# Layer 0 feed-forward on one core: rows normalised and scaled by ACT a tile ahead, first butterfly level taken by PE in pairs of blocks

## The chip, the core and the metric

The kernel runs on one core of a Trainium2 chip, as one launch. The metric is the device time of that launch in microseconds (us), lower being better. The engines are PE (TensorE, the matrix engine), DVE (VectorE), ACT (ScalarE), POOL (GpSimd) and SP (SyncE, which here only issues transfers). Each engine works through its own instructions in order. Engines wait for one another by semaphores that count up.

## What is computed

The whole kernel is four pairs of layers on x, 16 tiles of 128 rows by 256 columns. Each layer adds its result to x. This case is about the second of the eight, the feed-forward of layer 0, with a Hadamard transform and 8-bit quantised activations:

```python
def act_quant(x):                      # per row
    scale = 128 / clip(max(abs(x)), 1e-5)
    return clip(round(x * scale), -128, 127) / scale
def fwht(x):                           # over 1024 columns, h = 1, 2, 4, ... 512
    a, b = (x[..., 0, :], x[..., 1, :])
    x = stack([a + b, a - b])          # at each of ten levels
    return x / sqrt(1024)
n = layernorm(x)
gate = act_quant(n) @ weight_quant(w_gate).T      # 256 -> 1024
up   = act_quant(n) @ weight_quant(w_up).T
x = x + act_quant(fwht(silu(gate) * up)) @ weight_quant(w_down).T   # 1024 -> 256
```

The ten levels of the transform split in two: seven inside a block of 128 columns (one product with a 128x128 matrix of plus and minus ones, `had`), and three across the eight blocks (sums and differences of whole blocks, the "butterflies").

## The kernel before, in words

`hadamard_ffn` (from L1266 on) is the stage of this layer. It takes one tile of 128 rows after another, t = 0 to 15, in a pipeline that is written out by hand: each engine has a function `tile(t, u)` that lists what it does for which tile, and runs it for t = 0 to 15 (`over_long_pipe`; the last four tiles are written out, because there the work ahead falls away). u is t modulo 2 and picks one of two buffers. `ahead(t, n)` is true where tile t + n exists. What each engine does in its tile t, in this order:

- **DVE**: `quantise_x(t+3)`, which is normalise (L221), row maximum (L1348), its scale (L1350), reciprocal (L1352), `deq` (L1355), times the reciprocal plus a rounding constant (L1358), clip to bf16 (L1362); `gate_times_up(t+2)` (L1369, writes `prod`); `scale_h(t)`, which is the row maximum of the transformed tile in PSUM (L1374) and its scales down to the reciprocal `b_rec` (L1380); `add_to_x(t-1)` (L1390 and the row statistics, L193); `quantise_h(t)` (L1386).
- **ACT**: `copy_mixedT(t)` in two halves (L1434), `silu(t+2)` (L1428), `copy_hqT(t-1)` in two halves (L1447), `copy_xqT(t+3)` (L1421), `round_h(t)` (L1440).
- **PE**: `turn_mixed(t, 0)` (L1502), gate product of t+2 (L1491), `turn_mixed(t, 1)`, up product of t+2, `transform(t)` in two halves (L1511) with `turn_hq(t-1)` (L1526) behind each half, `turn_xq(t+3)` (L1480), `down(t-1)` (L1534).
- **POOL**: `butterflies(t)`: three levels of two instructions each (L1336, L1337), on halves of 128x512, prod to fly to prod to mixed.

The waits that matter below. `down(t-1)` waits until ACT has copied the turned rows of t+3 (`xqT_done`), since both use one bank of PSUM. `turn_mixed(t, 1)` waits for `copy_mixedT(t, 0)`, as there is one `ps_t`. `transform(t)` waits for both `copy_mixedT(t)` and for `round_h(t-1)`, as there is one `ps_f`. `scale_h(t)` waits for `had_put` of t. `add_to_x(t-1)` waits for `down(t-1)`.

Before the first tile POOL computes the reciprocal deviations of all 16 tiles (`all_rstd`, L216), then clears `zeros` and sets `magic`. DVE quantises rows 0, 1 and 2 between the first products.

Of the kernel before, what the change touches and what calls it, by code (L numbers as in the profile page):

```python
# [8 lines left out]
P = 128  # L9
# [49 lines left out]
        body(t, t % 2)  # L59


def over_ring(eng, body, n, ring, lead=1):

    rest = n % ring or ring
    for j in range(lead * ring):
        body(j, j % ring)
    with eng.Fori(lead, (n - rest) // ring) as i:
        for r in range(ring):
            body(i * ring + r, r)
    for j in range(n - rest, n):  # L70
# [25 lines left out]
class Core:  # L96


    def __init__(self, nc, ctx, dram):
# [32 lines left out]
        self.had = self.sb("had_matrix", [P, P], F32, self.early)  # L132
# [1133 lines left out]
def hadamard_ffn(core, name):  # L1266
# [3 lines left out]
    with core.stage() as st:  # L1270
        def sb(n, shape, dt=F32):
            return core.sb(f"{name}_{n}", shape, dt, st)

        def sem(n):
            return core.sem(f"{name}_{n}", st)
# [6 lines left out]
        xn = sb("xn", [P, D])  # L1282
        xq = sb("xq", [P, D], BF16)
        xqT = [sb(f"xqT{u}", [P, KC, P], BF16) for u in range(2)]
        a_max, a_rec = sb("a_max", [P, 1]), sb("a_rec", [P, 1])
# [5 lines left out]
        fly = sb("fly", [P, FF])  # L1291
# [19 lines left out]
        rstd_done = sem("rstd_done")  # L1311
        zeroed = sem("zeroed")
        block = st.enter_context(nc.Block())

# [5 lines left out]

        @block.gpsimd
        def _(pool):
            all_rstd(pool, core, rstd_done)
            pool.memset(core.zeros[:, :], 0.0).then_inc(zeroed, 1)
            pool.memset(magic[:, :], MAGIC).then_inc(const_done, 1)

            def butterflies(t, u):

                pool.wait_ge(prod_done, t + 1)
                if after(t, 2):  # L1330
                    pool.wait_ge(mixT_put, t - 1)
                for n, (src, dst) in enumerate(((prod[u], fly), (fly, prod[u]), (prod[u], mixed[u]))):
                    v, o = (m[:, :].rearrange("p (a two c) -> p a two c", two=2, c=P << n) for m in (src, dst))
                    if n:
                        pool.drain()
                    pool.tensor_tensor(o[:, :, 0, :], v[:, :, 0, :], v[:, :, 1, :], ALU.add)  # L1336
                    last = pool.tensor_tensor(o[:, :, 1, :], v[:, :, 0, :], v[:, :, 1, :], ALU.subtract)  # L1337
                last.then_inc(mixed_done, 1)

            over_tiles(pool, butterflies)  # L1340

        @block.vector
        def _(dve):
            def quantise_x(t, u):
                dve.drain()
                normalise(dve, core, xn[:, :], t)
                dve.drain()
                dve.tensor_reduce(a_max[:, :], xn[:, :], AX.X, ALU.max, apply_absolute_value=True)  # L1348
                dve.drain()
                dve.tensor_scalar(a_max[:, :], a_max[:, :], 1e-5, 1.0 / 128, ALU.max, ALU.mult)  # L1350
                dve.drain()
                dve.reciprocal(a_rec[:, :], a_max[:, :])  # L1352
                if after(t, 2):
                    dve.wait_ge(silu_done, t - 1)
                dve.tensor_scalar(deq[u][:, :], w_mean[:, 0:2], a_max[:, :], None, ALU.mult)\  # L1355
                   .then_inc(deq_done, 1)
                dve.drain()
                dve.tensor_scalar(xn[:, :], xn[:, :], a_rec[:, :], MAGIC, ALU.mult, ALU.add)  # L1358
                dve.drain()
                if after(t, 1):  # L1360
                    dve.wait_ge(xqT_put, t)
                dve.tensor_scalar(xq[:, :], xn[:, :], MAGIC, 127.0, ALU.subtract, ALU.min).then_inc(xq_done, 1)  # L1362

            def gate_times_up(t, u):
                dve.wait_ge(silu_done, t + 1)
                dve.wait_ge(up_put, t + 1)
                if after(t, 2):
                    dve.wait_ge(mixed_done, t - 1)
                dve.scalar_tensor_tensor(out=prod[u][:, :], in0=ps_u[:, :], scalar=deq[u][:, 1:2], in1=gate[:, :],  # L1369
                                         op0=ALU.mult, op1=ALU.mult).then_inc(prod_done, 1)  # L1370

            def scale_h(t, u):
                dve.wait_ge(had_put, t + 1)
                dve.tensor_reduce(b_max[:, :], ps_f[:, :], AX.X, ALU.max, apply_absolute_value=True)  # L1374
                dve.drain()

                dve.tensor_scalar(b_max[:, :], b_max[:, :], 32 * EPS_Q, 1.0 / 128, ALU.max, ALU.mult)
                dve.drain()
                dve.tensor_scalar(b_deq[u][:, :], b_max[:, :], w_mean[:, 2:3], 1.0 / 32, ALU.mult, ALU.mult)
                dve.reciprocal(b_rec[:, :], b_max[:, :]).then_inc(b_scale, 1)  # L1380

            def quantise_h(t):
                dve.wait_ge(round_done, t + 1)
                if after(t, 1):
                    dve.wait_ge(hqT_put, 2 * t)
                dve.tensor_scalar(hq[:, :], rounded[:, :], MAGIC, 127.0, ALU.subtract, ALU.min).then_inc(hq_done, 1)  # L1386

            def add_to_x(t, u):
                dve.wait_ge(y_put, t + 1)
                dve.scalar_tensor_tensor(out=core.xt(t), in0=ps_y, scalar=b_deq[u][:, :], in1=core.xt(t),  # L1390
                                         op0=ALU.mult, op1=ALU.add).then_inc(x_done, 1)
                dve.drain()
                row_stats(dve, core, t)

            def tile(t, u):
                if ahead(t, 3):
                    quantise_x(t + 3, 1 - u)
                if ahead(t, 2):
                    gate_times_up(t + 2, u)
                scale_h(t, u)  # L1400
                if after(t, 1):
                    add_to_x(t - 1, 1 - u)
                quantise_h(t)

            dve.wait_ge(rstd_done, 1)
            quantise_x(0, 0)
            quantise_x(1, 1)
            gate_times_up(0, 0)
            quantise_x(2, 0)
            gate_times_up(1, 1)  # L1410
            over_long_pipe(dve, tile)
            add_to_x(B - 1, 1)
            finish_stats(dve, core)

        @block.scalar
        def _(act):
# [55 lines left out]
        def _(pe):  # L1472
# [32 lines left out]
            def transform(t, half):  # L1505
# [1203 lines left out]
def lay_out(np, a):  # L2709
# [75 lines left out]
```

## Time and profile before

| | us |
|---|---|
| median of 3 runs | 1629.64 (1629.09 to 1630.54) |
| the profiled execution, its own time | 1628.51 |
| its span in the profile | 1626.7 |
| mean granted clock of TensorE, share of full | 0.936 |
| busy in the span: PE, DVE, ACT, POOL | 1352.0, 1071.2, 777.4, 631.9 |

The span is the time from the first to the last instruction of the profiled execution. The rest of its own time lies around it. A busy engine need not be what bounds a stage: what bounds it is read from which instruction starts as soon as which other one ends. "[x <-E y]" at the end of a row says that the engine had been idle for x us before it, until engine E had written y. Full clock of TensorE is 2.4 GHz; a granted clock of 0.50 is 1.2 GHz.

### The profile page before, as it was taken

How to read it: one execution, taken by the hardware profiler on the slowest of the kernel's cores; microseconds unless marked ns; L12 is line 12 of the kernel's file. 1: busy time of each engine (PE TensorE's matmuls, PEld its weight loads, DVE VectorE, ACT ScalarE, POOL GpSimd, SP SyncE). 2: the span in 40 equal slices, each digit the busy share in tenths (PEclk: the TensorE clock that was granted, in tenths of full speed). 3: DMA queues.
4: the chain of work that ended last, by engine and by line, in shares of the span. 5: the costliest groups of instructions: out<-in, count | busy, mean ns of one | idle time of the engine just before them, and what ended most of it. 6: DMA issues, size and time to landing. Idle time of an engine off the chain costs nothing. (4 is left out here: it accounts for less than half of the span.)

```text
span 1626.7 us, 29297 instructions
## 1 busy us (share of the span) xinstructions
PE 1352.0 (83%) x7976; PEld 845.5 (52%) x7992; DVE 1071.2 (66%) x2429; ACT 777.4 (48%) x2322; POOL 631.9 (39%) x649
## 2 busy tenths in 40 slices
PE   3899996566759969799997999978995999978993
PEld 2555553345534434476554666554663666654662
DVE  3898896788748855422664888875334888864224
ACT  2676773344540025432105888842442788833330
POOL 3112420777757523474002112112444665214661
PEclk9999997899979959999997999998998999998997
DMA  4231001400010022397501000141442210411224
GB/s 151 76 83 48 17 15 62 149 0 0 1 52 0 0 84 75 109 303 222 157 1 48 25 28 22 49 159 43 133 128 74 65 49 29 172 55 56 84 84 162
DMA packets 96447, 124.80 MB, mean 77 GB/s; under 512 B 11117, under 2 KB 76464, under 8 KB 96112
## 3 DMA queue, kind: packets, MB, share of 16 engines
q1 hardware_dynamic: 85392, 95.63, 18.5%
q0 software_dynamic: 10608, 28.07, 5.9%
q8 instruction: 36, 0.59, 0.1%
q14 instruction: 43, 0.35, 0.1%
q10 hardware_dynamic: 368, 0.16, 0.0%
HBM read 91.31 MB, written 33.43 MB: 77 GB/s over the span
## 5 line engine op out<-in xcount | busy, mean ns | idle before, releaser
L695 ACT ACTIVATE l0a_prob<-l0a_ps_s,l0a_neg_max 128x128 f32<-128x128 f32 x512 | 137.6, 398 | 67.7 <-DVE l0a_neg_max L553 60.0
L695 ACT ACTIVATE l2a_prob<-l2a_ps_s,l2a_neg_max 128x128 f32<-128x128 f32 x512 | 138.3, 399 | 26.7 <-DVE l2a_neg_max L553 21.7
L1135 ACT ACTIVATE l3a_prob<-l3a_ps_s,l3a_neg_max 128x256 f32<-128x256 f32 x256 | 104.3, 482 | 33.9 <-DVE l3a_neg_max L1050 32.3
L216 POOL TENSOR_TENSOR ln_rstd<-ln_var_eps,minus_half 128x16 f32<-128x16 f32 x7 | 20.5, 2922 | 233.5 <-POOLq L171 207.0
L553 DVE TENSOR_REDUCE l2a_neg_max<-l2a_ps_s 128x4 f32<-128x512 f32 x128 | 85.5, 683 | 19.1 <-PE l2a_ps_s L793 18.1
L501 POOL TENSOR_TENSOR l2a_k_head<-l2a_kT,head_of_row 128x512 f32<-128x512 f32 x32 | 32.9, 1047 | 161.7 <-DMA l2a_kT<-k_rows 161.7
L562 DVE COPY l0a_probT<-l0a_ps_t 128x512 f32<-128x512 f32 x128 | 84.4, 680 | 15.4 <-PE l0a_ps_t L805 15.2
L1050 DVE TENSOR_REDUCE l3a_neg_max<-l3a_ps_s 128x2 f32<-128x512 f32 x128 | 84.0, 679 | 14.2 <-PE l3a_ps_s L1186 13.0
L553 DVE TENSOR_REDUCE l0a_neg_max<-l0a_ps_s 128x4 f32<-128x512 f32 x128 | 85.2, 681 | 10.4 <-PE l0a_ps_s L793 9.6
L1748 PE MATMUL l1a_ps_y<-l1a_kv,l1a_tap 128*128 128x512 f32 x192 | 84.3, 602 | 3.7 <-POOL l1a_kv L1720 3.7
L501 POOL TENSOR_TENSOR l0a_k_head<-l0a_kT,head_of_row 128x512 f32<-128x512 f32 x30 | 30.8, 1047 | 145.6 <-DMA l0a_kT<-k_rows 145.6
L805 PE MATMUL l2a_ps_t<-ident,l2a_prob 128*128 128x128 f32 x512 | 75.6, 281 | 8.0 <-DVE l2a_probT L562 7.0
L805 PEld LDWEIGHTS l2a_ps_t<-ident,l2a_prob 128*128 128x128 f32 x512 | 56.7, 142 | 42.5 <-DVE l2a_probT L562 24.7
L2607 PE MATMUL l3f_ps_g<-l3f_w_gu_all,l3f_xinT 128*128 x156 | 73.5, 593 | 0.0
L805 PE MATMUL l0a_ps_t<-ident,l0a_prob 128*128 128x128 f32 x512 | 69.9, 273 | 1.8 <-DVE l0a_probT L562 1.8
L1198 PE MATMUL l3a_ps_t<-ident,l3a_prob 128*128 128x128 f32 x512 | 69.1, 278 | 2.2 <-ACT l3a_probT L1143 2.0
L1720 POOL TENSOR_TENSOR l1a_kv<-l1a_vT,ctxT_all 128x1024 f32 (+1 forms) x32 | 61.6, 1947 | 18.8 <-PE l1a_ps_y L1748 18.5
L2297 DVE TENSOR_TENSOR l3f_h_sb<-l3f_ps_g,l3f_act_sb 128x256 f32<-128x256 f32 x39 | 16.5, 424 | 77.9 <-ACT l3f_act_sb L2453 77.9
L562 DVE COPY l2a_probT<-l2a_ps_t 128x512 f32<-128x512 f32 x96 | 64.6, 681 | 4.4 <-PE l2a_ps_t L805 4.4
L783 PE MATMUL l0a_ps_s<-l0a_mask,identb 128*128 128x512 bf16 x128 | 49.7, 397 | 21.0 <-ACT l0a_prob L695 21.0
L2071 POOL DMA_INDIRECT l2f_xin<-expert_rows,l2f_tokens x47 | 44.6, 949 | 55.4 <-PE l2f_ps_x L2593 42.1
L1198 PEld LDWEIGHTS l3a_ps_t<-ident,l3a_prob 128*128 128x128 f32 x512 | 56.9, 142 | 17.1 <-ACT l3a_probT L1143 10.9
(477 smaller groups left out, 3532.4 us busy)
## 6 DMA issues: line engine op xcount, KB each, us to landing
l1f_w_gu<-in_l1f_w_gu SPq DMA_DIRECT2D x32, 352.0 KB, 6.8
expert_results<-zeros SPq DMA_DIRECT2D x1, 8320.0 KB, 26.3
l1f_got<-expert_results SPq DMA_DIRECT2D x16, 512.0 KB, 3.9
expert_results<-l2f_y_sb SPq DMA_DIRECT2D x47, 128.0 KB, 1.7
l1f_w_d<-in_l1f_w_d SPq DMA_DIRECT2D x32, 176.0 KB
l2f_w_gu_all<-in_l2f_w_gu SPq DMA_DIRECT2D x1, 4096.0 KB, 15.2
l3f_w_gu_all<-in_l3f_w_gu SPq DMA_DIRECT2D x1, 4096.0 KB, 15.4
l3f_got<-expert_results SPq DMA_DIRECT2D x16, 256.0 KB, 5.0
```

The costliest lines, as they stand in the source:

```text
L501: pool.tensor_tensor(k_head[u][:, c, :, :], kT[u][:, c:c + 1, :].broadcast_to([P, R, P]), core.head_of_row[:, :].unsqueeze(2).broadcast_to ...
L553: dve.tensor_reduce(neg_max[:, j, :], ps_s[j][:, :].rearrange("p (r k) -> p r k", r=R), AX.X, ALU.max, negate=True).then_inc(max_done, 1)
L562: dve.tensor_copy(probT[4 * c + j][:, :], ps_t[j % 2][:, :]).then_inc(t_done_v, 1)
L695: last = act.activation(prob[4 * c + j][:, r * P:r * P + P], ps_s[j][:, r * P:r * P + P], ACT.Exp, bias=neg_max[:, j, r:r + 1])
L783: pe.matmul(ps_s[j][:, :].rearrange("p (r k) -> p r k", r=R), core.identb[:, :], mask[u][:, :].unsqueeze(1).broadcast_to([P, R, P]), start ...
L805: last = pe.transpose(ps_t[j % 2][:, r * P:r * P + P], prob[4 * c + j][:, r * P:r * P + P], core.ident[:, :])
L1050: dve.tensor_reduce(neg_max[:, j, :], ps_s[j][:, :].rearrange("p (r k) -> p r k", r=2), AX.X, ALU.max, negate=True).then_inc(max_done, 1)
L1135: last = act.activation(prob[4 * c + j][:, m * D:m * D + D], ps_s[j][:, m * D:m * D + D], ACT.Exp, bias=neg_max[:, j, m:m + 1])
L1198: last = pe.transpose(ps_t[j % 2][:, k * D + m * P:k * D + m * P + P], prob[4 * c + j][:, m * D + k * P:m * D + k * P + P], core.ident[:, :])
L1720: pool.tensor_tensor(kv[u][:, c, :].rearrange("p (b j i) -> p b j i", b=B, i=N8), i_rows, j_rows, ALU.mult).then_inc(kv_done, 1)
L1748: last = pe.matmul(ps[u][c][:, cols], tap[u][:, (c - m) * P:(c - m) * P + P], kv[u][:, m, cols], start=(m == 0), stop=(m == c))
L2607: last = pe.matmul(ps_g[r % 2][:, 0:2 * FE], xinT[r % 2][:, c, :], w, start=(c == 0), stop=(c == KC - 1))
```

## The change

The normalising and the scaling of the rows move from DVE to ACT (`norm` writes `xn` a tile further ahead, `round_x` writes `xr`). DVE keeps the measuring (`measure_x`) and the clip (`clip_x`), which are put at other places of its tile. On POOL the level over neighbouring blocks goes; on PE each product with `had` has 256 columns in place of 128 and writes a pair of blocks, the second of the pair added to the first. POOL's first instruction is split, the first three tiles ahead of the rest. The long pipe has six tiles written out at its end in place of four.

```diff
@@ butterflies (POOL)
-                for n, (src, dst) in enumerate(((prod[u], fly), (fly, prod[u]), (prod[u], mixed[u]))):
+                for n, (src, dst) in ((1, (prod[u], fly[u])), (2, (fly[u], mixed[u]))):
...
@@ DVE
+            def shifts(lo, hi):
+                dve.scalar_tensor_tensor(out=shift[:, lo:hi], in0=core.stats[:, lo:hi, 0], scalar=-1.0, in1=core.rstd[:, lo:hi],
+                                         op0=ALU.mult, op1=ALU.mult).then_inc(shift_done, 1)
+            def measure_x(t, u):
+                dve.wait_ge(normed, t + 1)
+                dve.tensor_reduce(a_max[u][:, :], xn[u][:, :], AX.X, ALU.max, apply_absolute_value=True)
+                dve.drain()
+                dve.tensor_scalar(a_max[u][:, :], a_max[u][:, :], 1e-5, 1.0 / 128, ALU.max, ALU.mult)
+                dve.drain()
+                dve.reciprocal(a_rec[:, :], a_max[u][:, :]).then_inc(x_scaled, 1)
+                dve.tensor_scalar(deq[u][:, :], w_mean[:, 0:2], a_max[u][:, :], None, ALU.mult)\
                    .then_inc(deq_done, 1)
-                dve.drain()
-                dve.tensor_scalar(xn[:, :], xn[:, :], a_rec[:, :], MAGIC, ALU.mult, ALU.add)
-                dve.drain()
+            def clip_x(t):
+                dve.wait_ge(x_rounded, t + 1)
                 if after(t, 1):
                     dve.wait_ge(xqT_put, t)
-                dve.tensor_scalar(xq[:, :], xn[:, :], MAGIC, 127.0, ALU.subtract, ALU.min).then_inc(xq_done, 1)
+                dve.tensor_scalar(xq[:, :], xr[:, :], MAGIC, 127.0, ALU.subtract, ALU.min).then_inc(xq_done, 1)
...
             def tile(t, u):
-                if ahead(t, 3):
-                    quantise_x(t + 3, 1 - u)
                 if ahead(t, 2):
                     gate_times_up(t + 2, u)
                 scale_h(t, u)
+                if ahead(t, 3):
+                    clip_x(t + 3)
                 if after(t, 1):
                     add_to_x(t - 1, 1 - u)
+                if ahead(t, 4):
+                    measure_x(t + 4, u)
                 quantise_h(t)
...
@@ ACT
+            def norm(t, u):
+                act.activation(xn[u][:, :], core.xt(t), ACT.Identity, bias=shift[:, bass.ds(t, 1)],
+                               scale=core.rstd[:, bass.ds(t, 1)]).then_inc(normed, 1)
+            def round_x(t, u):
+                act.wait_ge(x_scaled, t + 1)
+                if after(t, 1):
+                    act.wait_ge(xq_done, t)
+                act.activation(xr[:, :], xn[u][:, :], ACT.Identity, bias=magic[:, :], scale=a_rec[:, :])\
+                    .then_inc(x_rounded, 1)
...
                 if ahead(t, 3):
                     copy_xqT(t + 3, 1 - u)
                 round_h(t)
+                if ahead(t, 4):
+                    round_x(t + 4, u)
+                if ahead(t, 5):
+                    norm(t + 5, 1 - u)
...
@@ PE, transform
                 for c in range(half * NF // 2, (half + 1) * NF // 2):
-                    last = pe.matmul(ps_f[:, c * P:c * P + P], mixedT[:, c * P:c * P + P], had[:, :], start=True, stop=True)
+                    odd = c % 2
+                    pair = slice((c - odd) * P, (c - odd + 2) * P)
+                    last = pe.matmul(ps_f[:, pair], mixedT[:, c * P:c * P + P], had[:, odd * P:(odd + 2) * P],
+                                     start=(odd == 0), stop=(odd == 1))
...
@@ lay_out
-    o["had"] = had
+    o["had"] = np.concatenate([had, had, -had], axis=1)
```

Before the pipe, in the new kernel, DVE measures and clips rows 0, 1 and 2 and measures row 3, and ACT norms rows 0 to 4 and rounds rows 0 to 3, between their copies and silus.

## Rows read from the trace of the kernel before

**Rows 1.** A steady stretch: us, each engine busy us (instructions), clock, DMA, GB/s
```profile
350.00:360.00 10.00, 6.42 (x52) 4.75 (x51) 8.53 (x16) 4.87 (x7) 7.92 (x7) 1.00 0.00 0
```

**Rows 2.** Timeline, DVE: start us, duration us; the maximum that opens scale_h
```profile
303.16 1.21 DVE L1374 TENSOR_REDUCE l0f_b_max<-l0f_ps_f 128x1 f32<-128x1024 f32 x1
...
354.02 1.21 DVE L1374 TENSOR_REDUCE l0f_b_max<-l0f_ps_f 128x1 f32<-128x1024 f32 x1
364.01 1.22 DVE L1374 TENSOR_REDUCE l0f_b_max<-l0f_ps_f 128x1 f32<-128x1024 f32 x1
...
424.29 1.21 DVE L1374 TENSOR_REDUCE l0f_b_max<-l0f_ps_f 128x1 f32<-128x1024 f32 x1
...
438.89 1.23 DVE L1374 TENSOR_REDUCE l0f_b_max<-l0f_ps_f 128x1 f32<-128x1024 f32 x1 [3.22 <-PE l0f_ps_f L1511]
```

**Rows 3.** Timeline, 351 to 361 us: work removed or moved, and what follows it
```profile
351.12 1.26 POOL L1337 TENSOR_TENSOR l0f_mixed<-l0f_prod 128x512 f32<-128x512 f32 x1
351.29 1.25 DVE L1358 TENSOR_SCALAR l0f_xn<-l0f_xn,l0f_a_rec 128x256 f32<-128x256 f32 x1
352.62 0.29 DVE L1362 TENSOR_SCALAR l0f_xq<-l0f_xn 128x256 bf16<-128x256 f32 x1
352.82 1.28 DVE L1369 SCALAR_TENSOR_TENSOR l0f_prod<-l0f_ps_u,l0f_deq,l0f_gate 128x1024 f32<-128x1024 f32 x1
353.89 1.03 PE L1534 MATMUL l0f_ps_q<-w_int,l0f_hqT 128*128 128x256 bf16 x8 [0.56 <-ACT l0f_xqT L1421]
354.18 1.26 POOL L1336 TENSOR_TENSOR l0f_fly<-l0f_prod 128x512 f32<-128x512 f32 x1 [1.79 <-DVE l0f_prod L1369]
...
355.67 0.15 DVE L1380 RECIPROCAL l0f_b_rec<-l0f_b_max 128x1 f32<-128x1 f32 x1
...
356.81 1.27 POOL L1336 TENSOR_TENSOR l0f_prod<-l0f_fly 128x512 f32<-128x512 f32 x1
...
358.99 0.92 DVE L221 TENSOR_SCALAR l0f_xn<-x_rows,ln_mean_var,ln_rstd 128x256 f32 x1 [0.36 <-issue]
...
359.98 0.42 DVE L1348 TENSOR_REDUCE l0f_a_max<-l0f_xn 128x1 f32<-128x256 f32 x1
...
360.70 0.17 DVE L1352 RECIPROCAL l0f_a_rec<-l0f_a_max 128x1 f32<-128x1 f32 x1
```

**Rows 4.** Timeline, last tiles, where DVE no longer quantises rows ahead
```profile
429.23 1.15 PE L1511 MATMUL l0f_ps_f<-had_matrix,l0f_mixedT 128*128 128x128 f32 x8
430.20 1.28 DVE L1369 SCALAR_TENSOR_TENSOR l0f_prod<-l0f_ps_u,l0f_deq,l0f_gate 128x1024 f32<-128x1024 f32 x1 [1.30 <-ACT l0f_gate L1428]
...
434.54 0.59 ACT L1434 ACTIVATE l0f_mixedT<-l0f_ps_t 128x512 f32<-128x512 f32 x1
...
436.52 1.16 PE L1511 MATMUL l0f_ps_f<-had_matrix,l0f_mixedT 128*128 128x128 f32 x8 [0.69 <-ACT l0f_mixedT L1434]
...
439.76 1.05 PE L1534 MATMUL l0f_ps_q<-w_int,l0f_hqT 128*128 128x256 bf16 x8 [0.69 <-ACT l0f_hqT L1447]
...
441.43 0.43 DVE L193 BATCH_NORM_STATS2 ln_partial<-x_rows 128x6 f32<-128x256 f32 x1
```

**Rows 5.** Instructions of a tile, next stage: ACT's norm, duration ns min/median/max
```profile
L1663 ACT ACTIVATE l1a_xn<-x_rows,l1a_shift,ln_rstd x16: 587/592/602, 460.3 to 476.3; 128x256 f32<-128x256 f32 x16
```

**Rows 6.** Last stage, fp32, 256 columns: one record, ns min/median/max; four, timeline
```profile
L2629 PE MATMUL l3f_ps_l<-l3f_w_d_all,l3f_hT_sb x152: 379/379/479, 1488.0 to 1599.0; 128*128 x152
...
1506.10 1.03 PE L2629 MATMUL l3f_ps_l<-l3f_w_d_all,l3f_hT_sb 128*128 x4
```

**Rows 7.** Stretches before and in a low clock, and the product in it
```profile
402.00:404.00 2.00, 0.28 (x2) 0.11 (x2) 1.92 (x3) 0.68 (x2) 0.54 (x1) 1.00 0.00 0
404.00:406.00 2.00, 1.96 (x10) 1.53 (x11) 1.85 (x5) 0.00 (x0) 1.58 (x2) 0.50 0.00 0
...
404.05 1.86 PE L1534 MATMUL l0f_ps_q<-w_int,l0f_hqT 128*128 128x256 bf16 x8 [0.57 <-ACT l0f_xqT L1421]
```

**Rows 8.** Timeline, the first transform of the stage
```profile
297.69 2.04 PE L1511 MATMUL l0f_ps_f<-had_matrix,l0f_mixedT 128*128 128x128 f32 x16
```

More of the change, by code:

```diff
@@ L59, in over_long_pipe, with over_x_pipe @@
         body(t, t % 2)
+def over_x_pipe(eng, body):
+    body(0, 0)
+    body(1, 1)
+    with eng.Fori(1, B // 2 - 3) as i:
+        body(i * 2, 0)
+        body(i * 2 + 1, 1)
+    for t in range(B - 6, B):
+        body(t, t % 2)
 def over_ring(eng, body, n, ring, lead=1):
@@ L90 @@
 READY = 3
+FIRST = 3
 RING = 4
@@ L131, in __init__ @@
         self.ffn_raw = [self.sb(f"ffn_raw{n}", [P, KC * FF], F32, self.early) for n in range(3)]
-        self.had = self.sb("had_matrix", [P, P], F32, self.early)
+        self.had = self.sb("had_matrix", [P, 3 * P], F32, self.early)
         self.w_int = [self.sb(f"w_int{n}", [P, KC * FF], BF16, self.early) for n in range(3)]
@@ L216, in all_rstd, with rstd_in_parts @@
     pool.tensor_tensor(core.rstd[:, :], core.var_eps[:, :], core.minus_half[:, :], ALU.pow).then_inc(done, 1)
+def rstd_in_parts(pool, core, done):
+    for part in (slice(0, FIRST), slice(FIRST, B)):
+        pool.tensor_tensor(core.rstd[:, part], core.var_eps[:, part], core.minus_half[:, part], ALU.pow).then_inc(done, 1)
 def normalise(dve, core, out, b):
@@ L1281, in hadamard_ffn @@
         magic = sb("magic", [P, 1])
-        xn = sb("xn", [P, D])
+        xn = [sb(f"xn{u}", [P, D]) for u in range(2)]
+        xr = sb("xr", [P, D])
+        shift = sb("shift", [P, B])
         xq = sb("xq", [P, D], BF16)
         xqT = [sb(f"xqT{u}", [P, KC, P], BF16) for u in range(2)]
-        a_max, a_rec = sb("a_max", [P, 1]), sb("a_rec", [P, 1])
+        a_max, a_rec = [sb(f"a_max{u}", [P, 1]) for u in range(2)], sb("a_rec", [P, 1])
         deq = [sb(f"deq{u}", [P, 2]) for u in range(2)]
@@ L1290, in hadamard_ffn @@
         prod = [sb(f"prod{u}", [P, FF]) for u in range(2)]
-        fly = sb("fly", [P, FF])
+        fly = [sb(f"fly{u}", [P, FF]) for u in range(2)]
         mixed = [sb(f"mixed{u}", [P, FF]) for u in range(2)]
@@ L1310, in hadamard_ffn @@
              "had_put", "b_scale", "round_done", "hq_done", "hqT_put", "hqT_done", "y_put", "x_done"))
-        rstd_done = sem("rstd_done")
+        rstd_done, shift_done, normed, x_scaled, x_rounded = (sem(n) for n in (
+            "rstd_done", "shift_done", "normed", "x_scaled", "x_rounded"))
         zeroed = sem("zeroed")
@@ L1322, in _ @@
         def _(pool):
-            all_rstd(pool, core, rstd_done)
+            rstd_in_parts(pool, core, rstd_done)
             pool.memset(core.zeros[:, :], 0.0).then_inc(zeroed, 1)
@@ L1331, in butterflies @@
                     pool.wait_ge(mixT_put, t - 1)
-                for n, (src, dst) in enumerate(((prod[u], fly), (fly, prod[u]), (prod[u], mixed[u]))):
+                for n, (src, dst) in ((1, (prod[u], fly[u])), (2, (fly[u], mixed[u]))):
                     v, o = (m[:, :].rearrange("p (a two c) -> p a two c", two=2, c=P << n) for m in (src, dst))
-                    if n:
+                    if n > 1:
                         pool.drain()
@@ L1343, in _ @@
         def _(dve):
-            def quantise_x(t, u):
+            def shifts(lo, hi):
[4 more added lines that the diff above has]
+                dve.tensor_reduce(a_max[u][:, :], xn[u][:, :], AX.X, ALU.max, apply_absolute_value=True)
                 dve.drain()
-                normalise(dve, core, xn[:, :], t)
+                dve.tensor_scalar(a_max[u][:, :], a_max[u][:, :], 1e-5, 1.0 / 128, ALU.max, ALU.mult)
                 dve.drain()
-                dve.tensor_reduce(a_max[:, :], xn[:, :], AX.X, ALU.max, apply_absolute_value=True)
-                dve.drain()
-                dve.tensor_scalar(a_max[:, :], a_max[:, :], 1e-5, 1.0 / 128, ALU.max, ALU.mult)
-                dve.drain()
[L1352 to L1355, printed above, removed]
+                dve.reciprocal(a_rec[:, :], a_max[u][:, :]).then_inc(x_scaled, 1)
+                dve.tensor_scalar(deq[u][:, :], w_mean[:, 0:2], a_max[u][:, :], None, ALU.mult)\
                    .then_inc(deq_done, 1)
-                dve.drain()
-                dve.tensor_scalar(xn[:, :], xn[:, :], a_rec[:, :], MAGIC, ALU.mult, ALU.add)
-                dve.drain()
+            def clip_x(t):
+                dve.wait_ge(x_rounded, t + 1)
                 if after(t, 1):
                     dve.wait_ge(xqT_put, t)
-                dve.tensor_scalar(xq[:, :], xn[:, :], MAGIC, 127.0, ALU.subtract, ALU.min).then_inc(xq_done, 1)
+                dve.tensor_scalar(xq[:, :], xr[:, :], MAGIC, 127.0, ALU.subtract, ALU.min).then_inc(xq_done, 1)
             def gate_times_up(t, u):
@@ L1400, in tile @@
                 scale_h(t, u)
+                if ahead(t, 3):
+                    clip_x(t + 3)
                 if after(t, 1):
                     add_to_x(t - 1, 1 - u)
+                if ahead(t, 4):
+                    measure_x(t + 4, u)
                 quantise_h(t)
             dve.wait_ge(rstd_done, 1)
-            quantise_x(0, 0)
-            quantise_x(1, 1)
+            shifts(0, FIRST)
+            measure_x(0, 0)
+            clip_x(0)
+            dve.wait_ge(rstd_done, 2)
+            shifts(FIRST, B)
+            measure_x(1, 1)
+            clip_x(1)
             gate_times_up(0, 0)
-            quantise_x(2, 0)
+            measure_x(2, 0)
+            clip_x(2)
             gate_times_up(1, 1)
-            over_long_pipe(dve, tile)
+            measure_x(3, 1)
+            over_x_pipe(dve, tile)
             add_to_x(B - 1, 1)
@@ L1459, in tile @@
                 round_h(t)
+                if ahead(t, 4):
+                    round_x(t + 4, u)
+                if ahead(t, 5):
+                    norm(t + 5, 1 - u)
+            act.wait_ge(shift_done, 1)
+            norm(0, 0)
+            norm(1, 1)
             act.wait_ge(const_done, 1)
+            round_x(0, 0)
+            round_x(1, 1)
             copy_xqT(0, 0)
+            norm(2, 0)
             copy_xqT(1, 1)
             silu(0, 0)
+            round_x(2, 0)
+            act.wait_ge(shift_done, 2)
+            norm(3, 1)
             copy_xqT(2, 0)
             silu(1, 1)
-            over_long_pipe(act, tile)
+            round_x(3, 1)
+            norm(4, 0)
+            over_x_pipe(act, tile)
             copy_hqT(B - 1, 0)
```

## The prediction

> **What bounds the kernel now.** Only the feed-forward of layer 0 changes, so its stage is read first by busy time and then in order of time. In a steady stretch of 10 us DVE is busy 8.53, POOL 7.92, PE 6.42 and ACT 4.87 us, at full clock [rows 1]. The maximum that opens `scale_h` comes once a tile, so its starts give the period: 354.02 to 364.01 is 10.0 us, and from 303.16 (tile 0) to 424.29 (tile 12) it is 121.1 us, 10.1 a tile [rows 2]. In these tiles DVE goes from one instruction to the next; it waits for nobody but shortly for `round_h`. Part of its time is lost to POOL: L1358 starts at 351.29 and ends at 352.54, and POOL's instruction beside it ends at 352.38, 0.16 us earlier [rows 3]. So DVE sets the period, its waits for POOL included. In the last tiles, where it quantises no rows ahead, the period is (438.89 - 424.29) / 2 = 7.3 us, and there DVE waits 3.22 us for the transform [rows 2]: the second bound is the chain transform, maximum, `round_h`, transform. From 303.16 to the start for tile 15 it is 135.7 + 7.3 = 143.0 us.
>
> **What is taken away.** DVE loses the normalise, 0.92 us, and the scaling, 1.25 us [rows 3], a tile: 2.2 us of 10. POOL loses two of six instructions of 1.26, so it can't bind. ACT gets two more instructions. The nearest row is `norm` of the next stage, the same operation on the same shape: 0.59 us [rows 5]. It has 4.87 + 1.18 = 6.05 us of work then, so by busy time it has room. By busy time alone the change would win. But the order in which the pieces were put back decides.
>
> **The new chain.** I follow what waits for what from the maximum of tile t to that of t+1, with time 0 at its start.
> - `b_rec` ends at 355.82 - 354.02 = 1.80 [rows 2, 3].
> - Only now comes `clip_x(t+3)` on DVE, 0.29 us, so 2.09 if nothing holds it. It stood ahead of `scale_h` before.
> - Does POOL hold it? POOL's work starts behind `gate_times_up(t+2)`, which starts when `silu` is done, 430.20 - 429.23 = 0.97 after the transform's start, and takes 1.28 [rows 4]. POOL follows 0.08 later; its third instruction starts 356.81 - 354.18 = 2.63 behind the first and takes 1.27 [rows 3]. So it ends 6.23 us after the transform's start, and the clip, 0.16 behind it as L1358 was, at 6.39.
> - The transform. Each of its 16 records a tile goes from 128 to 256 columns. 16 took 2.04 [rows 8]; at 256 columns four took 1.03 and one 0.38, so the step is (1.03 - 0.38) / 3 = 0.217 and 16 take 3.63 [rows 6]. That is 1.6 more. From its start to the maximum it was 438.89 - 436.52 = 2.37 [rows 2, 4]; it becomes 3.97. The clip ends at 6.39 - 3.97 = 2.42.
> - `turn_xq(t+3)`, the copy `copy_xqT(t+3)`, then `down(t-1)`, which waits for that copy: from the clip's end to the start of `down` 353.89 - 352.91 = 0.98 [rows 3]. At 3.40.
> - `down(t-1)` and then `add_to_x(t-1)` with its statistics: 441.86 - 439.76 = 2.10 [rows 4]. At 5.50. Before, this lay beside DVE's queue and cost nothing; its cover was the rows work that stood ahead.
> - `measure_x(t+4)` is queued behind it: maximum to reciprocal 360.87 - 359.98 = 0.89 [rows 3], and 0.07 of gap. At 6.46.
> - `round_x(t+4)` waits for that, in ACT's order behind `round_h(t)`, and behind it are `norm(t+5)` and `copy_mixedT(t+1, 0)`. 0.05 + 2 x 0.59 = 1.23. At 7.69. This is the added wait that matters: all of ACT's next tile is queued behind it, and PE's second `turn_mixed` and its transform wait for ACT.
> - From `copy_mixedT(t+1, 0)` to the next transform 436.52 - 434.54 = 1.98 [rows 4]. At 9.67.
> - The transform, 3.97. The next maximum starts at **13.64**.
>
> Each link is an order of one engine or a semaphore, and each comes once in a tile, so the period can't be under this sum at these prices, however free DVE is. The period of 10.0 becomes 13.6.
>
> **The sum.** Tiles 0 to 10: 11 x 13.64 = 150.0. Tile 11 has no `norm` behind it, 13.05. Tile 12 has the clip but no `round_x`: `down` ends at 4.43, `turn_mixed` at about 5.0 (half of the tile's product of 1.15 [rows 4]), then 1.98 and 3.97: 11.0. Tiles 13 and 14: 7.3 + 1.6 = 8.9 each. Together 191.9 against 143.0: +48.9. Before the pipe: the first transform ended at 299.73 and its maximum started at 303.16 [rows 2, 8], held by the rows of tile 3 on DVE. That 3.4 goes, 1.6 of wider products and up to 1.2 for `round_x(3)` and `norm(4)` ahead of ACT's first copy come, and the clips of the first rows are held less; -4 to +1, I take -2. The split of POOL's first instruction and DVE's `shifts` are in this bound. Longer buffers and the larger `had` load lie far ahead and cost nothing: the load is issued in an earlier stage.
>
> The clock. In 402 to 404 PE had 0.28 us of work, and from 404 on the granted clock was 0.50, the 1.2 GHz level; `down` then took 1.86 in place of 1.03 [rows 3, 7]. It cost nothing there, as DVE set the period. Now PE idles twice in a tile: from the transform's end to `down` (0 to 3.4, but for 0.28 of work), and from the gate product (about 6) until ACT's copy is done (8.3). I expect one fall a tile, seen on `down`: 0.83 x 12 = +10. Bounds: 0 where the clock holds; 0.83 and half of a transform at half speed, 1.8, so 2.6 a tile, +32.
>
> +48.9 - 2 + 10 = +57 on the profiled execution's 1628.5: 1685.4. The median of the runs is 1.1 above that execution, so **1686** for the median.
>
> What the Trainium skill would put here: "TensorE: Matmul & The Clock Gate", section "Wait — 56ns, not 53.3ns?", has back-to-back products N / 2.4 GHz + 2.5 ns apart, and the footnote of "Perfetto Trace Analysis" halves the rate for fp32 in two parts. By that a record goes from 112 to 218 ns, 1.7 us a tile in place of 1.6, since the pages leave out the weight load beside it. It would make the sum some 1.5 us larger. The 0.217 of the row agrees with its 218.
>
> **The rivals.**
> - *DVE's relief comes through* (chance 0.06). ACT would have to be let go early: `x_scaled` of t+4 at or before the end of `round_h(t)`, about 4.5 (clip end 2.42, copy done about 3.3, `round_h` 1.2), and not at 6.46. Then the chain is clip, copy, `round_h`, transform: 4.5 + 3.97 = 8.5. 12 x (8.5 - 10.1) = -19, three last tiles at +1.6, -2 before the pipe: -16, so 1614. For it speaks that DVE is the busiest engine now. It decides only if the part from `down` to `copy_mixedT` loses over 3.6 us of its length, which is where the period passes 10.0; the order written in `tile` speaks against that. "SBUF — State Buffer", section "Who interferes with whom", of the Trainium skill says that ACT never waits for another engine's port, which speaks for this side: the two instructions moved there lose their waits for POOL. The trace's even 587 to 602 ns of `norm` agrees [rows 5]. It says nothing of the queue.
> - *The clock holds* (0.20): the same chain without the 10, 1676.
> - *The clock falls in both gaps* (0.15): +32 in place of +10, 1708.
> - *A shorter chain* (0.07): the clip finds POOL between instructions (-0.3 a tile), `round_x` and `norm` overlap or take less (-0.4), or wide products cost half of what I take, all at full clock: 12 x 1 to 1.5 less than 1676, 1658 to 1664.
> - *No difference* (0.02): the two sides would have to cancel.
>
> The forecast itself has 0.50. The range is 1665 to 1708: the forecast with the bounds of its unknown prices and both clock rivals. Changes of 0.2% (3.3 us) are about the least that a measurement of this kernel can tell. Faster 0.06, within 0.02, slower 0.92.
>
> **What would show it.** Right: maxima (L1374 before) about 13.6 to 14.5 us apart, DVE idle before them with the transform as releaser; ACT idle some 2 us before `round_x` on the reciprocal; DVE idle before `add_to_x` on `down`; DVE's busy time a tile near 6 us; 16 records of 256 columns in 3.6 us. The stage longer, every other stage as before. Wrong: a period under 10, or ACT's `round_x` with no idle time before it, would refute the chain. A granted clock of 1.0 throughout the stage gives the second rival.

## The result, and the profile of the changed kernel

The changed kernel took 1688.41 us (median of 4 runs, 1678.55 to 1695.31) against 1629.91 before: a ratio of 1.0344, 95% interval [1.0298, 1.0391]. The forecast was 1686. The profiled execution took 1691.74 us with a span of 1690.0 (before 1628.51 and 1626.7).

First the steady part of the stage, from the first maximum (tile 0) to that of tile 11 in the changed kernel, and to that of tile 12 in the one before. The columns are stretch, its length, busy time and instructions of PE, PE's weight loads, DVE, ACT and POOL, then granted clock, DMA share, GB/s.

```profile
301.28:465.02 163.74, 116.62 (x542) 78.81 (x542) 64.77 (x141) 63.57 (x98) 56.41 (x46) 0.79 0.01 4
```

That is 163.74 / 11 = 14.9 us a tile, where the kernel before took 10.1. The kernel before:

```profile
303.16:424.29 121.13, 81.85 (x582) 60.50 (x595) 104.02 (x180) 58.44 (x84) 96.34 (x74) 0.94 0.00 0
```

DVE worked 104.02 / 12 = 8.7 us a tile and now 64.77 / 11 = 5.9: the relief came. POOL went from 8.0 to 5.1, ACT from 4.9 to 5.8. No engine is short of time, and the tile is 4.8 us longer. PE's busy share is no measure here: its busy time grew with wide products and with the low clock (0.79 in place of 0.94). Now the starts of the maximum that opens `scale_h`, DVE's timeline:

```profile
301.28 1.22 DVE L1395 TENSOR_REDUCE l0f_b_max<-l0f_ps_f 128x1 f32<-128x1024 f32 x1 [1.49 <-PE l0f_ps_f L1569]
314.67 1.23 DVE L1395 TENSOR_REDUCE l0f_b_max<-l0f_ps_f 128x1 f32<-128x1024 f32 x1 [3.09 <-PE l0f_ps_f L1569]
328.12 1.23 DVE L1395 TENSOR_REDUCE l0f_b_max<-l0f_ps_f 128x1 f32<-128x1024 f32 x1 [1.68 <-PE l0f_ps_f L1569]
342.29 1.22 DVE L1395 TENSOR_REDUCE l0f_b_max<-l0f_ps_f 128x1 f32<-128x1024 f32 x1 [1.68 <-PE l0f_ps_f L1569]
356.80 1.23 DVE L1395 TENSOR_REDUCE l0f_b_max<-l0f_ps_f 128x1 f32<-128x1024 f32 x1 [1.68 <-PE l0f_ps_f L1569]
372.99 1.22 DVE L1395 TENSOR_REDUCE l0f_b_max<-l0f_ps_f 128x1 f32<-128x1024 f32 x1 [2.70 <-PE l0f_ps_f L1569]
...
465.02 1.22 DVE L1395 TENSOR_REDUCE l0f_b_max<-l0f_ps_f 128x1 f32<-128x1024 f32 x1 [2.93 <-PE l0f_ps_f L1569]
...
508.99 1.22 DVE L1395 TENSOR_REDUCE l0f_b_max<-l0f_ps_f 128x1 f32<-128x1024 f32 x1 [5.19 <-PE l0f_ps_f L1569]
```

These answer to [rows 2]. The first periods are 13.4, 13.5 and 14.2 us, later ones 14.5 and 16.2 by turns. DVE is idle ahead of each maximum and is released by the transform; before it was so in the last two tiles alone. From the first to the last maximum it is 508.99 - 301.28 = 207.7 us against 143.0; that and the earlier start, 301.28 against 303.16, make +62.8 of the 63.3 us by which the span grew. The other stages kept their length.

One tile in order of time, 328.12 to 342.29, the chain that the prediction built from [rows 3] and [rows 4]:

```profile
329.24 1.26 POOL L1357 TENSOR_TENSOR l0f_mixed<-l0f_fly 128x512 f32<-128x512 f32 x1
...
329.78 0.15 DVE L1401 RECIPROCAL l0f_b_rec<-l0f_b_max 128x1 f32<-128x1 f32 x1
329.86 0.79 DVE L1383 TENSOR_SCALAR l0f_xq<-l0f_xr 128x256 bf16<-128x256 f32 x1
...
331.10 0.38 ACT L1462 ACTIVATE l0f_xqT<-l0f_ps_q 128x256 bf16<-128x256 bf16 x1 [2.16 <-PE l0f_ps_q L1536]
331.62 1.57 PE L1593 MATMUL l0f_ps_q<-w_int,l0f_hqT 128*128 128x256 bf16 x8 [0.56 <-ACT l0f_xqT L1462]
...
333.36 0.48 DVE L1411 SCALAR_TENSOR_TENSOR x_rows<-l0f_ps_q,l0f_b_deq,x_rows 128x256 f32 x1 [2.72 <-PE l0f_ps_q L1593]
...
335.08 0.16 DVE L1375 RECIPROCAL l0f_a_rec<-l0f_a_max 128x1 f32<-128x1 f32 x1
...
335.28 0.60 ACT L1455 ACTIVATE l0f_xr<-l0f_xn,l0f_magic,l0f_a_rec 128x256 f32<-128x256 f32 x1 [2.70 <-DVE l0f_a_rec L1375]
335.79 0.58 ACT L1448 ACTIVATE l0f_xn<-x_rows,l0f_shift,ln_rstd 128x256 f32 x1
336.28 0.57 ACT L1475 ACTIVATE l0f_mixedT<-l0f_ps_t 128x512 f32<-128x512 f32 x1
...
337.60 0.60 ACT L1475 ACTIVATE l0f_mixedT<-l0f_ps_t 128x512 f32<-128x512 f32 x1 [0.75 <-PE l0f_ps_t L1558]
...
338.26 1.98 PE L1569 MATMUL l0f_ps_f<-had_matrix,l0f_mixedT 128*128 128x256 f32 x8
```

What to see is that one link follows the other without a break, across engines. The clip lasts until POOL's third instruction is done (329.24 to 330.50) and ends at 330.65, `down` starts at 331.62, the sum into x at 333.36, behind it the reciprocal of the rows ahead ends at 335.24, ACT's `round_x` has been idle for 2.70 us and starts at 335.28, `norm` follows, then the first copy of the turned tile at 336.28, and PE's transform at 338.26. Two of the longest waits of the stage (engine, tile, releaser, total us, times, longest):

```profile
DVE x_rows L1411 <- PE l0f_ps_q L1593: 34.8, 12, 3.1
...
ACT l0f_xr L1455 <- DVE l0f_a_rec L1375: 31.6, 11, 3.1
```

The second is the new one: 11 tiles, some 2.9 us each, with all of ACT's next tile queued behind it.

### The profile page after: what moved, and what is told of

Read it like the earlier page. It is cut to its first block and busy times, and to the rows that moved or that the text cites. A ratio compares the mean times of both kernels' runs of the same rounds, so it can differ in the third digit from the quotient of the medians.

```text
span 1690.0 us, 29216 instructions
## 1 busy us (share of the span) xinstructions
PE 1407.5 (83%) x7991; PEld 875.8 (52%) x7992; DVE 1029.5 (61%) x2399; ACT 793.2 (47%) x2354; POOL 586.9 (35%) x618
## 5 line engine op out<-in xcount | busy, mean ns | idle before, releaser
L713 ACT ACTIVATE l2a_prob<-l2a_ps_s,l2a_neg_max 128x128 f32<-128x128 f32 x512 | 138.3, 401 | 26.3 <-DVE l2a_neg_max L571 21.5
L580 DVE COPY l0a_probT<-l0a_ps_t 128x512 f32<-128x512 f32 x128 | 84.4, 680 | 15.4 <-PE l0a_ps_t L823 15.3
L1357 POOL TENSOR_TENSOR l0f_fly<-l0f_prod 128x512 f32<-128x512 f32 x16 | 20.2, 1266 | 134.6 <-DVE l0f_prod L1390 134.6
L1569 PE MATMUL l0f_ps_f<-had_matrix,l0f_mixedT 128*128 128x256 f32 x256 | 64.9, 398 | 1.4 <-ACT l0f_mixedT L1475 1.4
## 6 DMA issues: line engine op xcount, KB each, us to landing
l2f_w_gu_all<-in_l2f_w_gu SPq DMA_DIRECT2D x1, 4096.0 KB, 14.5
l3f_w_gu_all<-in_l3f_w_gu SPq DMA_DIRECT2D x1, 4096.0 KB, 14.9
```

The costliest lines, as they stand in the source:

```text
L580: dve.tensor_copy(probT[4 * c + j][:, :], ps_t[j % 2][:, :]).then_inc(t_done_v, 1)
L713: last = act.activation(prob[4 * c + j][:, r * P:r * P + P], ps_s[j][:, r * P:r * P + P], ACT.Exp, bias=neg_max[:, j, r:r + 1])
L1569: last = pe.matmul(ps_f[:, pair], mixedT[:, c * P:c * P + P], had[:, odd * P:(odd + 2) * P], start=(odd == 0), stop=(odd == 1))
```

## The experiments

The chips differ in the time of the kernel before (1631.6, 1650.2 and 1635.2 us, medians, for the three groups of four), so what is compared is the ratio to the runs of before beside it. "Stage" is the time from the first to the sixteenth maximum in the profile, 143.0 us before and 207.7 after. The chain theory says that the order of the pieces sets the period. Its rival says that the work added to PE and ACT does.

**One link taken out.** DVE measures ahead of the sum into x.

```diff
-                if after(t, 1):
-                    add_to_x(t - 1, 1 - u)
                 if ahead(t, 4):
                     measure_x(t + 4, u)
+                if after(t, 1):
+                    add_to_x(t - 1, 1 - u)
```

> One swap in the changed kernel: DVE measures the rows of t+4 before it adds tile t-1 to x. Chain theory: the reciprocal then comes about 3.4 us after the maximum instead of 6.5, ACT's round_h ends at 4.5, round_x and norm at 5.7, so the period at full clock goes from 13.6 to about 11.7 us and the time from 1688 to about 1666 us (the same loss to the clock). Rival, that PE's wider products and its low clock set the time and not the order: no change, 1680 to 1695 us.

Measured 1665.69 us, ratio 1.0201 [1.0134, 1.0267], stage 175.8, periods of 11.3 and 12.6 by turns, granted clock in the stage 0.91. ACT's timeline:

```profile
403.36 1.20 ACT L1481 ACTIVATE l0f_rounded<-l0f_ps_f,l0f_magic,l0f_b_rec 128x1024 f32<-128x1024 f32 x1
404.45 0.60 ACT L1455 ACTIVATE l0f_xr<-l0f_xn,l0f_magic,l0f_a_rec 128x256 f32<-128x256 f32 x1
404.94 0.59 ACT L1448 ACTIVATE l0f_xn<-x_rows,l0f_shift,ln_rstd 128x256 f32 x1
405.43 0.59 ACT L1475 ACTIVATE l0f_mixedT<-l0f_ps_t 128x512 f32<-128x512 f32 x1
```

No idle time is left ahead of L1455: `round_x`, `norm` and the copy follow `round_h` without a break. The periods of 11.3 are those at full clock, a little under the 11.7 expected. Two swapped lines gave back 22 us. Part of that can be the clock (0.82 in the first profile of the changed kernel), but not all: with the clock at 0.99 the old order still takes 189.2 us for the stage (last run of this part), 13.4 more than this one. So the rival, no change, is refuted.

**ACT's rows a tile later.** They stand behind `silu` of the next tile; the two that stood ahead of the pipe, for tiles 3 and 4, go, as the pipe now does them.

```diff
                     silu(t + 2, u)
+                if ahead(t, 3):
+                    round_x(t + 3, 1 - u)
+                if ahead(t, 4):
+                    norm(t + 4, u)
...
                 round_h(t)
-                if ahead(t, 4):
-                    round_x(t + 4, u)
-                if ahead(t, 5):
-                    norm(t + 5, 1 - u)
```

> ACT's round_x and norm move from the end of its tile to behind silu of the next tile, where their input has been ready for long; nothing else. Chain theory: ACT copies the turned tile as soon as round_h and PE's turn_mixed (behind down) are done, period about 11.0 us at full clock, 1688 - 12 x 2.6 = about 1657 us. Rival, that PE's wider products and its low clock set the time: no change, 1680 to 1695 us.

Measured 1661.30 us, ratio 1.0181 [1.0108, 1.0254], stage 179.0. Periods of 10.95 and 10.97 where the clock holds, up to 13.6 where it doesn't (0.87 over the stage; 0.75 in the tile of 13.63). The chain's 11.0 is met, in two periods, and more of the time went to the clock than I had put.

**And the clip back ahead of scale_h.**

```diff
+                if ahead(t, 3):
+                    clip_x(t + 3)
                 scale_h(t, u)
-                if ahead(t, 3):
-                    clip_x(t + 3)
```

> As the run with ACT's rows moved behind silu, and DVE's clip goes back ahead of scale_h. Chain theory: no row work is left between the maximum and the next transform; 1.8 + 1.2 + 2.0 + 4.0 = 9.0 us a tile, under the 10.0 of the kernel before, and three last tiles at +1.6: about 1619 us, faster than before. Rival, that ACT's and PE's extra work is what costs: slower than before, 1640 us or more.

Measured 1619.06 us, ratio 0.9921 [0.9892, 0.9950], stage 138.3, all steady periods 9.26 or 9.27, clock 1.00. Again on another chip:

> The kernel with rows on ACT in the good order and the butterfly level on PE, again: period 9.27 us, ratio to before 0.992 to 0.996, so about 1% slower than the run beside it with the level on POOL. If the two tie, the wide products cost nothing in the good order.

1619.94 us, ratio 0.9906 [0.9873, 0.9939], just under the expected range, the same periods. So all of the change's work in another order is faster than the kernel before. One period of the first of these two runs, in order of time:

```profile
373.47 1.23 DVE L1395 TENSOR_REDUCE l0f_b_max<-l0f_ps_f 128x1 f32<-128x1024 f32 x1 [1.48 <-PE l0f_ps_f L1567]
375.32 1.20 ACT L1481 ACTIVATE l0f_rounded<-l0f_ps_f,l0f_magic,l0f_b_rec 128x1024 f32<-128x1024 f32 x1 [0.27 <-DVE l0f_b_rec L1401]
...
376.70 0.60 ACT L1475 ACTIVATE l0f_mixedT<-l0f_ps_t 128x512 f32<-128x512 f32 x1 [0.18 <-PE l0f_ps_t L1556]
...
378.71 1.98 PE L1567 MATMUL l0f_ps_f<-had_matrix,l0f_mixedT 128*128 128x256 f32 x8
...
382.73 1.23 DVE L1395 TENSOR_REDUCE l0f_b_max<-l0f_ps_f 128x1 f32<-128x1024 f32 x1 [1.48 <-PE l0f_ps_f L1567]
```

Between two maxima stand `round_h`, copy and transform alone. The copy starts 0.18 us later than `round_h` ends, since PE's turn of the tile waits for `down`; that is most of the 0.27 us over the 9.0 of the forecast.

**The second half of the change alone** (the kernel before, with the butterfly level on PE):

> The kernel before with the second half of the change alone: the neighbouring-block level on PE over 256 columns, four POOL instructions in place of six; the rows stay on DVE ahead of gate_times_up. Chain theory: no new wait, so DVE still sets the period and gains what it no longer waits for POOL (its clip and scaling find POOL idle): about 9.4 us a tile in place of 10.0, last three tiles +1.6 each: about 1627 us. Rival, that the wide products are the cost of the change: slower than before, 1640 us or more.

Ratio 0.9959 [0.9908, 1.0010] (1643.28 us, with 1650.18 before on that chip), stage 139.9, periods 9.0 to 9.5. In time it can't be told from no change; the stage is 3.1 us shorter. The two instructions whose wait for POOL the prediction measured, in DVE's timeline:

```profile
374.19 0.41 DVE L221 TENSOR_SCALAR l0f_xn<-x_rows,ln_mean_var,ln_rstd 128x256 f32 x1 [0.36 <-issue]
...
375.83 0.35 DVE L1358 TENSOR_SCALAR l0f_xn<-l0f_xn,l0f_a_rec 128x256 f32<-128x256 f32 x1
```

0.41 and 0.35 us against 0.92 and 1.25 [rows 3]: with two POOL instructions fewer they meet no POOL instruction. That relief pays for the wider products and a little more. In the old order of the rows they are no loss.

**The first half alone** (the changed kernel, products of 128 columns and six POOL instructions):

> The changed kernel with the butterfly level back on POOL and products of 128 columns: only the rows' move to ACT in the changed order. Chain theory: the same chain without the 1.6 us of wider products, about 12.2 us a tile at full clock and some 1 us more for the low clock, so about 1666 us, still far above before. Rival, that the wide products are the cost: about 1630 us or less.

Ratio 1.0230 [1.0182, 1.0279] (1689.03 us, 1650.18 before), stage 186.7, clock 0.83, periods 13.0 to 14.4. The expected number came from 12.2 + 1; the ratio meets it (1.0230 x 1629.9 = 1667). The steady periods, 13.7 on average, are above the 13.2 expected, so that the ratio meets the number is partly luck. Most of the loss stands without the wide products. The rest, from 1.0230 to the 1.0335 to 1.0344 of the whole change, some 17 to 19 us, is what they cost on this chain.

**The good order without the second half.**

> The kernel of the 1619 us run (ACT's rows behind silu, clip ahead of scale_h) with the butterfly level back on POOL and products of 128 columns. Chain theory: the chain maximum, round_h, transform is 7.4 us and POOL's six instructions with their waits about 8.0 to 8.5, so POOL sets the period at about 8.3: about 1601 us. Rival, that the butterfly on PE is needed to let DVE go on, as POOL's instructions hold DVE's: 1619 us or more.

Ratio 0.9872 [0.9827, 0.9916] (1630.15 us, 1650.18 before), stage 123.2, eleven periods of 8.29 or 8.30. The period is the one expected; the ratio would be 1609 us on the first chip, 8 more than expected. Again, on a chip with the changed kernel and with the good order and wide products beside it:

> The kernel with rows on ACT in the good order and the butterfly level on POOL, again: period 8.30 us, ratio to before 0.985 to 0.990. Against the same order with the butterfly on PE: 12 x (9.27 - 8.30) and three tiles at 1.6 less, about 15 us faster, if the stage's difference reaches the end of the kernel.

1607.02 us, ratio 0.9827 [0.9789, 0.9865], 12.9 us under the 1619.94 of the wide products (15 expected), and a ratio just under the expected range. It beats both kernels. One period in the first of the two runs, POOL and the two DVE instructions that meet it:

```profile
377.21 1.27 POOL L1357 TENSOR_TENSOR l0f_fly<-l0f_prod 128x512 f32<-128x512 f32 x1
...
378.43 1.27 POOL L1358 TENSOR_TENSOR l0f_fly<-l0f_prod 128x512 f32<-128x512 f32 x1
...
379.84 1.27 POOL L1357 TENSOR_TENSOR l0f_prod<-l0f_fly 128x512 f32<-128x512 f32 x1
...
381.05 0.68 DVE L1407 TENSOR_SCALAR l0f_hq<-l0f_rounded 128x1024 bf16<-128x1024 f32 x1
381.07 1.80 POOL L1358 TENSOR_TENSOR l0f_prod<-l0f_fly 128x512 f32<-128x512 f32 x1
...
383.00 1.27 POOL L1357 TENSOR_TENSOR l0f_mixed<-l0f_prod 128x512 f32<-128x512 f32 x1
383.16 1.26 DVE L1383 TENSOR_SCALAR l0f_xq<-l0f_xr 128x256 bf16<-128x256 f32 x1
...
384.23 1.31 POOL L1358 TENSOR_TENSOR l0f_mixed<-l0f_prod 128x512 f32<-128x512 f32 x1
...
385.50 1.26 POOL L1357 TENSOR_TENSOR l0f_fly<-l0f_prod 128x512 f32<-128x512 f32 x1
```

From 377.21 to 385.50 is one period, 8.29 us. POOL goes from one instruction to the next; the gaps of 0.13 us are the drains between the levels. Its fourth instruction takes 1.80 in place of 1.27, beside DVE's L1407, and DVE's clip takes 1.26 in place of 0.29, beside POOL's fifth. POOL sets this period, as forecast.

**The clock.** The changed kernel again gives the spread:

> The changed kernel as it is, on one chip with the next three, for their comparison: ratio to before 1.03 to 1.04. Periods of 13.6 us where the clock holds and 14.5 to 16.2 where it falls.

1688.45 us, ratio 1.0335 [1.0294, 1.0377], stage 198.7 with a clock of 0.88 (207.7 with 0.82 in the first profile). The same program, so 9 us of the stage differ with the clock alone. Where it falls, in the first profile:

```profile
362.00:366.00 4.00, 2.85 (x11) 1.33 (x9) 2.27 (x7) 1.57 (x3) 0.00 (x0) 0.50 0.00 0
366.00:370.00 4.00, 4.00 (x13) 2.79 (x14) 0.99 (x1) 1.60 (x2) 0.00 (x0) 0.56 0.00 0
370.00:374.00 4.00, 3.18 (x21) 2.51 (x19) 1.30 (x2) 1.19 (x2) 3.49 (x3) 1.00 0.00 0
```

The clock is at 0.50 (1.2 GHz) here and comes back in the transform. It was there already in the short turn ahead of `down`, which takes 0.39 us in place of 0.28. The instructions of that tile:

```profile
359.45 0.39 PE L1536 MATMUL l0f_ps_q<-identb,l0f_xq 128*128 128x128 bf16 x2 [2.47 <-DVE l0f_xq L1383]
...
360.41 1.87 PE L1593 MATMUL l0f_ps_q<-w_int,l0f_hqT 128*128 128x256 bf16 x8 [0.57 <-ACT l0f_xqT L1462]
...
365.99 1.12 PE L1558 MATMUL l0f_ps_t<-ident,l0f_mixed 128*128 128x128 f32 x4 [1.15 <-ACT l0f_mixedT L1475]
...
366.89 1.91 PE L1547 MATMUL l0f_ps_u<-w_int,l0f_xqT 128*128 128x512 bf16 x4
...
368.60 2.35 PE L1569 MATMUL l0f_ps_f<-had_matrix,l0f_mixedT 128*128 128x256 f32 x8
```

`down` takes 1.87 us in place of 1.03, the second turn of the tile 1.12 in place of 0.66, the up product 1.91 in place of 1.03, half of the transform 2.35 in place of 1.98. Together that is some 2.5 us on the chain, and this period is 16.2. In the next, 14.6 us, only `down` is slow (1.86). So I filled PE's gaps with products whose result is overwritten. In the second gap (between gate product and second turn):

```diff
                     if ahead(t, 2):
                         gate_up(t + 2, u, half)
+                    if half == 0 and after(t, 1):
+                        pe.wait_ge(round_done, t)
+                        keep_busy(pe, core, ps_f, 9)
```

> The changed kernel with nine products more a tile on PE (128x512 bf16, 0.22 us each at full clock, result overwritten), put into the gap between the gate product and the second turn_mixed, while PE waits for ACT. If the low clock costs what the periods of 14.5 and 16.2 us show over 13.6, and comes from this gap, the periods fall to 13.6 to 14.2 us and the time to about 1678 us although PE does more. If the clock has no part: 1688 us or more.

1689.37 us, ratio 1.0346 [1.0277, 1.0416], periods 13.3 to 15.7: a miss, no gain. The clock did rise, to 0.92 over the stage, and five periods are at full clock, 13.3 to 13.7 us. In the others it still falls ahead of `down` or in it, and in the tile of 15.7 the filling itself is slow (2.75 us in place of 2.11) and holds up the turn behind it. It also costs in the last tiles (10.4 in place of 9.0 us). Then both gaps, only where they exist:

> The changed kernel with nine products more in each of PE's two gaps (behind the last turn_hq, and behind the gate product), only in the tiles that have both gaps. If the low clock is the rest of the loss over the chain: the granted clock stays at or near 1.00 in the stage, all steady periods are 13.6 to 13.8 us, and the time is about 1676 us although PE has the more work. If the fall came from something else: periods over 14 us remain, 1685 us or more.

Ratio 1.0271 [1.0225, 1.0318] (1695.44 us, 1650.18 before; as 1674 on 1629.9), stage 189.7, clock 0.99, steady periods 13.5 to 13.7. And the first gap alone, behind the last `turn_hq`:

```diff
+                if ahead(t, 3):
+                    keep_busy(pe, core, ps_t, 9)
                 if ahead(t, 3):
                     turn_xq(t + 3, 1 - u)
```

> The changed kernel with nine products more a tile in the first gap alone (behind the last turn_hq), in the tiles that have it. Theory that both gaps let the clock fall, each in its turn: the granted clock of the stage is between that of the changed kernel (0.82) and that with both filled (0.99), periods mixed between 13.6 and 15.5, some 6 us faster than the changed kernel. Rival, that the first gap alone is the cause: all periods 13.6, 12 us or more faster.

1672.66 us, ratio 1.0243 [1.0200, 1.0285], so 15.8 us under the changed kernel beside it. The whole stage (columns as above), and PE in one tile:

```profile
302.49:491.70 189.21, 144.78 (x839) 97.08 (x837) 81.09 (x178) 80.84 (x123) 68.21 (x55) 0.99 0.00 1
```

```profile
370.80 1.03 PE L1593 MATMUL l0f_ps_q<-w_int,l0f_hqT 128*128 128x256 bf16 x8 [0.57 <-ACT l0f_xqT L1462]
...
375.52 0.66 PE L1558 MATMUL l0f_ps_t<-ident,l0f_mixed 128*128 128x128 f32 x4 [2.39 <-ACT l0f_mixedT L1475]
...
376.87 1.98 PE L1569 MATMUL l0f_ps_f<-had_matrix,l0f_mixedT 128*128 128x256 f32 x8
...
380.92 2.11 PE L199 MATMUL l0f_ps_t<-identb 128*128 128x512 bf16 x9
```

Clock 0.99, steady periods 13.5 to 13.7. The second gap is open (2.39 us idle ahead of L1558) and the transform behind it runs at full clock. My expectation, both gaps in turn with some 6 us gained, fell; the numbers are those of its rival, all periods near 13.6 and over 12 us gained. It also shows the chain by itself: 13.6 us a tile with the full clock. That the second gap never lets the clock fall doesn't follow. In the second profile of the changed kernel, in the period of 15.3 us:

```profile
343.88 1.03 PE L1593 MATMUL l0f_ps_q<-w_int,l0f_hqT 128*128 128x256 bf16 x8 [0.56 <-ACT l0f_xqT L1462]
...
348.75 0.66 PE L1558 MATMUL l0f_ps_t<-ident,l0f_mixed 128*128 128x128 f32 x4 [2.54 <-ACT l0f_mixedT L1475]
...
349.25 1.69 PE L1547 MATMUL l0f_ps_u<-w_int,l0f_xqT 128*128 128x512 bf16 x4
```

Here the clock held over the first gap, `down` took 1.03 us, and it fell behind the second: the up product took 1.69 in place of 1.03, half of the transform 2.96 in place of 1.98.

## Why the prediction was right

- **The bound before** and the relief: right. DVE's time a tile fell by 2.8 us, more than the 2.2 counted, as the waits for POOL went too, and it bought nothing.
- **The chain**: forecast 13.64; the run with the first gap filled has 13.5 to 13.7. Link by link, in the tile of 328.12: clip ends at 2.53 (forecast 2.42), `down` starts at 3.50 (3.40), maximum from the transform's start 4.03 (3.97), copy to transform 1.98 (1.98). One link was too long: `round_x` and `norm` take 0.60 and 0.58, but start 0.51 and 0.49 us apart, so ACT's part is 1.0 and not 1.23. In the run at full clock it was made up by tenths elsewhere, partly by luck. In the tile shown `down` ran in part at the low clock (1.57 us), which is why everything from there on is late.
- **That the order and not the work is the price**: shown. Two orders changed (the first three runs) take the ratio from 1.034 to 0.992 with the same instructions. What the work costs depends on the order: the wide products are worth 1.0 to 1.1% on the changed kernel's chain, 0.8% in the good order, and nothing with the rows left on DVE.
- **The transform at 256 columns**: 1.6 us forecast; two halves of 1.98 and 1.95, where 1.16 and 1.11 stood before, is 1.66.
- **The clip's wait for POOL**: right in its place; 0.79 us for an instruction of 0.29.
- **Ahead of the first maximum**: -2 forecast, 301.28 - 303.16 = -1.9 in the first profile, -2.6 in the second.
- **The clock**: right in kind and too small. I took +10; in the first profile it is 207.7 - 189.2 = 18.5 us, in the second 9.5, and 15.8 between the medians side by side. What was mis-sized is the number of things that run slowly: I priced `down` alone, but the second turn, the up product and the start of the transform are hit too. The chain at full clock came out smaller than forecast, 189.2 against 191.9, above all because tile 0, which has no `down` of a tile before it, takes 10.8 us where 13.64 was put (the last period takes 10.7 where 8.9 was put). The two errors offset in part: the stage grew by 64.7 us, where 48.9 + 10 was forecast.
- **The closeness of the number** is partly luck. The profiled execution was forecast at 1685.4 and took 1691.74, 6.3 more. It was one of the slower ones, so the median, 1688.41, lies nearer to the 1686.
- **The rivals**: the faster one fails at the point that was named, `x_scaled` (6.46 forecast; 335.24 - 328.12 = 7.12). Its mechanism is real: let ACT go, and the kernel is faster, which the third run shows. That the clock holds didn't happen (0.82 and 0.88 over the stage); where the filling makes it hold, the ratio of 1.0243 is 1669.5 us on the first chip, against that rival's 1676. The full +32 of a fall in both gaps didn't come, though single tiles come near it. The rule of the Trainium skill, "SBUF — State Buffer", section "Who interferes with whom", is that ACT never waits for another engine's port; this trace agrees with it (`norm` 584 to 599 ns in this stage), and it did not decide.

## What to carry to other kernels

Work taken from the busiest engine of a hand-written pipeline is worth what the slot is worth where it is put back. Write the new chain out from one tile's milestone to the next with each engine's order as a link, before busy times are believed; a piece that needs a result of this tile must not stand ahead of one that the next tile needs. And once the order is right, ask again which engine is short: here the butterfly level was better left on POOL.

## What was not expected

Filling one of PE's two idle gaps a tile was enough. In the changed kernel the first is 2.5 us idle, then a turn of 0.28 to 0.39, then 0.57 idle. With it filled the second, 2.39 us, stayed open, and in the steady tiles the clock never fell; it fell once, in the last tiles, which have no filling. Filling the second alone kept the clock up in five tiles and gained nothing. But with neither filled the clock has also fallen behind the second (the period of 15.3 us above). So the first gap matters more, and what each adds to the other was not tried. Nine unused products a tile (2.1 us of PE's work) made the kernel some 16 us faster. And the good order with the wide products keeps the clock at 1.00 over the whole stage with no filling at all, so a part of its gain over the changed kernel is the clock's.
